# Second attention of a two-layer transformer kernel: one of each group's 24 turned units is copied out of PSUM by ACT instead of DVE

## The reference

```python
q = rmsnorm(hidden_states @ wq_a.T, q_a_ln_w) @ wq_b.T      # 16 heads, 128 + 64 (rotary)
ckv = hidden_states @ wkv_a.T                                # 64 latent + 64 rotary, shared by all heads
q_abs = jnp.einsum('bhsd,hdc->bhsc', q_nope, q_absorb)
scores = (jnp.einsum('bhsc,btc->bhst', q_abs, kv) + jnp.einsum('bhsd,bxtd->bhst', q_pe, k_pe)) * SCALE
scores = jnp.where(causal, scores, jnp.finfo(scores.dtype).min)
attn = jax.nn.softmax(scores, axis=-1)
x = jnp.einsum('bhst,btc->bhsc', attn, kv)                   # then out_absorb and wo
```

## Time and profile before

| | us |
|---|---|
| runs: median (lowest, highest) | 1298.84 (1294.29, 1300.28) |
| profiled execution, its own time | 1293.62 |
| span in it, first to last instruction | 1291.8 |
| PE busy in the span | 1178.7 (91%) |
| DVE busy | 905.9 (70%) |
| ACT busy | 744.9 (58%) |
| POOL busy | 552.4 (43%) |

### The profile page before, as it was taken

The page is one execution under the profiler, slowest core; times in us unless marked ns, Lnnn a source line. Parts: engine busy times, 40 slices in busy tenths (PEclk is TensorE's granted clock), DMA queues, the critical chain, the costliest instruction groups (busy, mean ns, idle before and its releaser), DMA issues.

```text
span 1291.8 us, 22469 instructions
## 1 busy us (share of the span) xinstructions
PE 1178.7 (91%) x7552; PEld 842.2 (65%) x7552; DVE 905.9 (70%) x2340; ACT 744.9 (58%) x1668; POOL 552.4 (43%) x567
## 2 busy tenths in 40 slices
PE   3888698999999888899899999999999999999998
PEld 3776653444443576778677767777767776777688
DVE  7867698899997254566666777666777666777744
ACT  2467326777777235454566666656666656666632
POOL 2336434444341101536445565554565554565310
PEclk9899958999999988899899999999999999999999
DMA  6774154466620474031210111111101310101315
GB/s 195 141 148 77 49 68 59 60 95 91 77 47 2 136 209 140 1 105 65 74 46 17 39 37 45 46 46 30 33 31 45 111 46 17 50 26 53 112 50 179
DMA packets 112467, 93.55 MB, mean 72 GB/s; under 512 B 49697, under 2 KB 102241, under 8 KB 110561
## 3 DMA queue, kind: packets, MB, share of 16 engines
q1 hardware_dynamic: 112352, 92.11, 30.6%
HBM read 53.02 MB, written 30.67 MB: 65 GB/s over the span
## 4 chain that ended last, share of the span: by engine, by line
PE 36%; DVE 12%; issue 3%; ACT 1%; DMA 0%; ACTq 0%; DVEq 0%
PE psum L1049 11%; PE psum L1097 9%; PE psum L194 8%; PE psum L1070 7%; DVE a_part L962 3%; DVE psum L967 3%; DVE a_pt L1000 3%; DVE w L2337 1%; ACT a_p L1014 1%; DVE w_lat L2337 1%; DVE q00l L2337 1%; DVE q01l L2337 1%; DVE a_nm L967 1%; DMA w<-wf_d 0%; DVE ql1l L2218 0%
## 5 line engine op out<-in xcount | busy, mean ns | idle before, releaser
L1031 POOL TENSOR_SCALAR a_p<-a_p,a_rl 128x128 f32<-128x128 f32 (+7 forms) x256 | 218.2, 854 | 300.3 <-DVE a_rl L973 300.3
L1014 ACT ACTIVATE a_p<-psum,a_nm 128x128 f32<-128x128 f32 (+7 forms) x256 | 189.4, 740 | 55.7 <-DVE a_nm L967 54.1
L1532 ACT ACTIVATE a_pt<-psum 128x512 f32<-128x512 f32 (+3 forms) x384 | 167.7, 493 | 71.6 <-PE psum L1395 68.4
L1000 DVE COPY a_pt<-psum 128x512 f32<-128x512 f32 (+1 forms) x192 | 114.5, 596 | 109.0 <-PE psum L1070 108.6
L1070 PE MATMUL psum<-ident,a_p 128*128 128x128 f32 x1152 | 175.4, 279 | 14.2 <-DVE a_pt L1000 14.2
L998 ACT ACTIVATE a_pt<-psum 128x256 f32<-128x256 f32 (+2 forms) x192 | 87.5, 455 | 164.3 <-PE psum L1070 164.2
L1070 PEld LDWEIGHTS psum<-ident,a_p 128*128 128x128 f32 x1152 | 127.2, 140 | 62.3 <-issue 47.8
L1097 PE MATMUL psum<-a_pt,v 128*64 128x256 f32 (+1 forms) x1280 | 159.4, 370 | 1.4 <-ACT rows_k L1111 1.4
L1385 PE MATMUL psum<-a_op_k,a_op_q 64*128 64x512 f32 (+3 forms) x384 | 135.9, 451 | 9.0 <-ACT a_op_q L1551 7.9
L1395 PE MATMUL psum<-a_op_q,a_op_k 64*128 64x512 f32 (+3 forms) x384 | 128.0, 413 | 8.4 <-ACT a_pt L1532 6.9
L1395 PEld LDWEIGHTS psum<-a_op_q,a_op_k 64*128 64x128 f32 x384 | 63.0, 193 | 101.8 <-ACT a_pt L1532 84.8
(11 more groups left out here) (389 smaller groups left out, 2878.6 us busy)
## 6 DMA issues: line engine op xcount, KB each, us to landing
ot_d<-rows_k SPq DMA_DIRECT2D x16, 512.0 KB, 3.0
a_swap<-w_p SPq DMA_DIRECT2D x60, 128.0 KB, 2.3
rows_q<-qk_d SPq DMA_DIRECT2D x48, 128.0 KB, 4.6
rows_k<-qk_d SPq DMA_DIRECT2D x48, 128.0 KB, 7.8
w<-wf_d SPq DMA_DIRECT2D x15, 384.0 KB, 3.4
qk_d<-d_stage_h SPq DMA_DIRECT2D x64, 64.0 KB, 2.1
qk_d<-d_stage_l SPq DMA_DIRECT2D x64, 64.0 KB, 2.1
d_x<-in_L_attn_x_dram SPq DMA_DIRECT2D x8, 256.0 KB, 6.8
```

Of the source, the lines that this page charges most:

```text
L1000: e.tensor_copy(dst, src).then_inc(mine, 1)
L1014: e.activation(s.p[:, t % NPB, 0:(i + 1) * P], C.score[t % 2][:, 0:(i + 1) * P], ACT.Exp, scale=-1.0, bias=s.nm[:, k:k + 1], accum_out=s.l ...
L1031: e.tensor_scalar(s.p[:, t % NPB, 0:(i + 1) * P], s.p[:, t % NPB, 0:(i + 1) * P], s.rl[:, k:k + 1], 1.0, ALU.mult, ALU.mult).then_inc(s.no ...
L1532: e.activation(pt[:, k // G0 % NPT, hd, off:HALF], bank_b("score", g, k)[:, off:HALF], ACT.Exp, scale=-1.0).then_inc(exped, 1)
```

## The change

Units with U % 24 == 12, that is U12 of each group, are copied by ACT, in its slot 14 ahead of U13, and no longer by DVE in its slot 15. `by_act` says which units are ACT's, `copied(U, act)` how many of the units below U an engine has copied, and the waits use these counts. The bank of a unit stays that of its parity. `multiply` waits for both engines' last copies at pairs 5 and 6. Two semaphores of the first layer are cleared by POOL at the end of the first attention.

```diff
+    def by_act(self, U):
+
+        return U % 2 == 1 or U % self.UG == self.unit0(self.SG - LAG - 2)
+
+    def copied(self, U, act):
+
+        return sum(self.by_act(x) == act for x in range(U % self.UG)) + U // self.UG * sum(
+            self.by_act(x) == act for x in range(self.UG))
...
     for w in range(core.n_units(i)):
-        if (u0 + w) % 2 != parity:
+        U = n * 2 * core.UG + u0 + w
+        if core.by_act(U) != bool(parity):
             continue
-        U = n * 2 * core.UG + u0 + w
...
-        src = C.turn[parity][:, 0:(k1 - k0) * P].rearrange("p (k q) -> p k q", q=P)
+        src = C.turn[U % 2][:, 0:(k1 - k0) * P].rearrange("p (k q) -> p k q", q=P)
...
-                par = (u0 + w) % 2
-                if later or u0 + w >= 2:
-                    e.wait_ge(s.ev_act if par else s.ev_dve, n * core.UG + (u0 + w) // 2)
+                par = U % 2
+                if U >= 2:
+                    e.wait_ge(s.ev_act if core.by_act(U - 2) else s.ev_dve, core.copied(U - 1, core.by_act(U - 2)))
...
-            e.wait_ge(s.ev_dve, n * core.UG + (U + 1) // 2)
-            e.wait_ge(s.ev_act, n * core.UG + U // 2)
+            e.wait_ge(s.ev_dve, core.copied(U, False))
+            e.wait_ge(s.ev_act, core.copied(U, True))
...
-        elif p == 5:
-            e.wait_ge(s.ev_dve, half_units)
-        elif p == 6:
-            e.wait_ge(s.ev_act, half_units)
+        elif p <= 6:
+            e.wait_ge(s.ev_dve, s.core.copied(all_units, False))
+            e.wait_ge(s.ev_act, s.core.copied(all_units, True))
...
                 attend0(nc, C, qk_d, v_d, ot, m_d, N, (w1, w2, w3), rows_in)
+                for sem in raw_in:
+                    nc.gpsimd.sem_clear(range(sem.num, sem.num + 1))
```

More of the change, by code:

```diff
@@ L1086, in value_pe @@
         if j == 0:
-            U = core.unit0(tt % core.SI) + core.units[tt % core.SG] + (0 if tt >= 0 else -2 * core.UG)
-            e.wait_ge(s.ev_dve, n * core.UG + (U + 1) // 2)
-            e.wait_ge(s.ev_act, n * core.UG + U // 2)
+            U = core.unit0(tt % core.SI) + core.units[tt % core.SG] + (2 * n if tt >= 0 else 2 * n - 2) * core.UG
+            e.wait_ge(s.ev_dve, core.copied(U, False))
+            e.wait_ge(s.ev_act, core.copied(U, True))
             if later or cc >= len(C.out):
@@ L2157, in output1 @@
     w_high, w_low, high, low, used, added, out = (ph.sem(n) for n in ("w_high", "w_low", "high", "low", "used", "added", "out"))
-    NG, half_units = B * NG1, B * NG1 // 2 * s.core.UG
+    NG, all_units = B * NG1, B * NG1 * s.core.UG
     pairs = len(units) // 2
```

## The result

The changed kernel took 1285.52 us in the median of five runs (1280.97 to 1287.16), against 1296.21 us of the kernel before in five: a ratio of 0.9879, with a 95% interval of 0.9852 to 0.9906. The medians are 10.7 us apart here, 15.1 and 10.3 in the other two. Forecast were 1285.3 us and 13.5 us less, a ratio of 0.990.

A forecast was written before the change was run, and what follows sets the result against it. The prediction took the DVE, ACT, PE path to slot 1's scores in the second attention as the bound. 15 groups x 0.85 + 0.76 = 13.5 us off the 1298.84 us median gave 1285.3 us, range 1279 to 1291.5.

The forecast's parts named there:

- What bounds: Second attention, each group's end: path DVE, ACT, PE to slot 1's scores counts; PE's 0.84 us copy wait is a side branch.
- DVE's step: DVE loses U12's copy: reduction 0.57 us earlier, U14's copy 0.85 us earlier, not waiting for PE.
- ACT and PE behind it: Step 15's mask, exponential and PE's slot 1 scores follow 0.85 us earlier; PE's wait there grows from 0.27 to 0.43 us.
- ACT's step: ACT gains U12's copy: step 14's exponential later, PE waiting 0.1 to 0.3 us, covered in slot 1 and costed at nothing.
- The last group: No exponential holds PE after the last group; its transposes start at 1229.17 instead of 1229.93: 0.76 us gained.
- The sum: Second attention: 15 x 0.85 + 0.76 = 13.5 us gained, giving 1285.3 us, 1.0% less.
- B: DVE starts each instruction only when the one before has ended: 0.66 us a group, 10.7 us gained, 1288.1 us; 14%.
- C: The wait moves to step 14's exponential, behind ACT's copies of U12 and U13: gain gone, 1296 to 1299 us; 7%.
- D: Slower: ACT copies U12 late, delaying U13's copy and step 14's exponential, and PE behind step 15: 1305 us; 3%.
- E: Change doesn't do what it says: PE's 0.84 us wait stays under ACT's name, 1297 to 1299 us; 5%.

The follow-up runs named there:

- the other two: The unedited changed kernel compared twice more with the kernel before: ratios 0.9894 and 0.9916.
- experiments 2: Against the changed kernel: ACT copies U14 instead of U12, which DVE keeps in its late place; ratio 0.9934 to the kernel before, 38.05 us a group.
- experiment 5: Against experiment 1: U12's early DVE copy also goes ahead of the reciprocal that releases POOL's product; ratio 0.9937 to the kernel before, 38.28 us a group.
- Experiment 1: Against the changed kernel: U12 stays on DVE, copied in slot 14 ahead of the 64 x 1024 subtraction; ratio 1.0038 to the kernel before, 38.96 us a group.
- experiments 6: Against the changed kernel: one useless ACT copy a group between U13's copy and step 14's exponential; 1275.63 us in one run, 37.70 us a group.
- experiment 7: Against the changed kernel: three useless ACT copies a group between U13's copy and step 14's exponential; 1296.39 us in one run, 38.70 us a group.
- experiment 11: Against the changed kernel: ACT copies U10 and U14 as well as U12; ratio 0.9836 to the kernel before, 37.23 us a group.

## Why the prediction was right

*What bounds.* That PE's visible wait is a side branch, and that the start of the scores in slot 1 is what counts, is shown by experiments 2 and 5 from two sides: a gain without the visible wait getting shorter, and PE free 0.66 us sooner for a gain of 0.30. Experiment 1 doesn't add to it, as PE stood just as long there.

*DVE's step.* From the subtraction's start the reduction was forecast 1.15 us on and came 1.14 us on, U14's copy 1.76 and 1.75, the mask 2.37 and 2.35. The gain was put at 0.85 us and measured 0.88; the copy did not wait for PE.

*ACT and PE behind it.* PE's wait for step 15's exponential was to be 0.43 us and is 0.41.

*ACT's step.* U12's copy started 0.35 us ahead of the subtraction, as forecast. The exponential of step 14 was to come 0.39 to 0.50 us later and came 0.20 later (0.30 us behind the subtraction's start, against 0.10). The term was mis-sized: I carried on the 0.34 us from U13's copy to that exponential, part of which was a wait for the bias and no distance (its read by DVE ended at 920.31 + 0.14 = 920.45, 0.03 us before). PE did not wait at all for this one, where 0.1 to 0.3 us were allowed for. It had no weight in the sum, and experiments 6 and 7 show the cover on which that rested.

*The last group.* Its transposes now start 0.23 us behind the last score product:

```profile
1221.64 0.39 PE L1058 MATMUL psum<-k11l,w 128*128 128x512 f32 x1
1221.87 0.82 PE L1079 MATMUL psum<-ident,a_p 128*128 128x128 f32 x6
```

It was 0.99: 0.76 us, as forecast.

*The sum.* 15 x 0.88 + 0.76 = 14.0 us, all of what the second attention lost, against 13.5. That the median came out within 0.3 us of the forecast is partly luck: the forecast stood on a median of three that was 2.6 us above that of five. The ratio is the fair comparison, and 0.990 lies within each of the three intervals. The gains in medians, 10.7, 15.1 and 10.3 us, lie on both sides of 13.5.

*The rivals.* B falls: the reduction starts at 921.29, 0.06 us before the subtraction's end at 921.35, and the mask at 922.50 where that rule would have it at 921.35 + 0.69 + 0.68 = 922.72. The sentence of the Trainium skill by which B was costed ("VectorE: DVE Perf Modes", "The DRAIN you can't avoid") has an exception right behind it, a next instruction that is not held starts earlier, and the trace agrees with the exception by these 0.06 us. C and D did not occur; experiment 7 is C made by hand, from 1.68 us of extra work. E falls with the rows of ACT.

## What to carry to other kernels

Where an engine in the chain reports a wait, ask what its next meeting point with the same chain is: moving the late copy forward on DVE freed PE 0.66 us sooner and was worth 0.30 us, leaving PE's wait and shortening the other branch 0.53, moving U12 to ACT, which does both, 0.88. In a loop, the distance between two marks of a group, over many groups, resolves 0.01 us where whole runs scatter by several.
An instruction that is moved also moves what it releases: here one reciprocal, ahead of a subtraction and not right before it, started another engine first and cost 0.68 us a group. And a wait that is gone at one place can stand at the next, so look at the whole stretch up to the meeting point.

## What was not expected of the hardware

DVE's subtraction of two SBUF tensors (64 x 1024) and POOL's product over SBUF (128 x 1024) slow each other down here. Which of them started first decided: DVE first, 1.20 and 1.89 or 1.91 us (kernel before, experiment 5); POOL first by 0.29 us, 1.12 and 1.90 us (experiment 1). The second one loses about 0.7 to 0.8 us. In experiment 11, where DVE started 0.01 us ahead, they took 1.25 and 2.16 us. The Trainium skill has this in "SBUF — State Buffer", section "Who interferes with whom": a DVE instruction with two SBUF inputs contends with a GpSimd instruction that reads SBUF, and the order of issue decides who is blocked. The trace agrees. I had the 1.89 us in the trace of before and did not put it into experiment 1's number.
